# Low target blocks of a graph network's last five layers: sums by gathered rows beside the dense products

## The reference

```python
# second layer (l1 in the kernel): both directions of each edge, unit weights
src2, dst2 = concat([src, dst, loop]), concat([dst, src, loop])
agg = segment_sum(x[src2] * dis[src2] * dis[dst2], dst2);  x = layernorm(x + relu(agg @ W.T + bias))
# third (l2): one direction, unit weights
out = segment_sum((x @ W)[row] * dinv[row] * dinv[col], col) + b;  x = layernorm(x + prelu(out))
# fourth to sixth (l3a, l3b, l3c): one direction, edge weights; 128 -> 256 -> 256 -> 128 features
h = relu(conv(x, W1));  h = relu(conv(h, W2));  x = layernorm(x + conv(h, W3))
```

## Time and profile before

| what | value |
|---|---|
| median of 3 runs | 5592.74 us (5584.71 to 5594.79) |
| time of the profiled execution | 5637.0 us |
| its span from first to last instruction | 5635.2 us |
| TensorE (PE) busy | 4813.6 us, 85% |
| VectorE (DVE) busy | 2493.0 us, 44% |
| GpSimd (POOL) busy | 1199.1 us, 21%, all but 5 us in the first layer |
| moved to and from HBM | 1178.49 MB, 209 GB/s |
| granted clock of TensorE over the span | 0.910 of full speed |

### The profile page before, as it was taken

One profiled execution on the slowest core, in us unless ns is written; L12 is line 12 of the kernel. 1 busy time (PEld: TensorE's weight loads), 2 busy tenths in 40 slices (PEclk: granted clock), 3 DMA queues, 4 the chain that ended last, 5 costly groups with the idle time before them and its releaser, 6 DMA issues. The chain is left out here.

```text
span 5635.2 us, 75975 instructions
## 1 busy us (share of the span) xinstructions
PE 4813.6 (85%) x30664; PEld 3047.7 (54%) x30664; DVE 2493.0 (44%) x4225; ACT 1157.3 (21%) x2219; POOL 1199.1 (21%) x845
## 2 busy tenths in 40 slices
PE   3788888888888863388879989999999999999999
PEld 2777777777777753233334444444444444454444
DVE  5877888888788767755542220111000000001111
ACT  0555555555555541100000000000000000000000
POOL 2655656566666610000000000000000000000000
PEclk6888988889898876689989999999999999999999
DMA  4665666666666651288876658887444444338887
GB/s 139 204 199 188 218 198 202 205 202 216 199 213 213 201 179 55 94 299 294 298 225 206 212 187 305 305 306 263 150 155 144 147 149 155 140 132 289 310 306 261
DMA packets 689173, 1178.49 MB, mean 209 GB/s; under 512 B 77284, under 2 KB 450384, under 8 KB 688440
## 3 DMA queue, kind: packets, MB, share of 16 engines
q1 hardware_dynamic: 617004, 1079.58, 55.6%
q0 software_dynamic: 26864, 55.10, 3.9%
q10 hardware_dynamic: 44956, 38.94, 2.2%
HBM read 823.64 MB, written 349.75 MB: 208 GB/s over the span
## 5 line engine op out<-in xcount | busy, mean ns | idle before, releaser
L756 POOL DMA_INDIRECT x<-p_table,src_i x832 | 1191.9, 1433 | 801.6 <-DVE x L553 516.3
L1197 PE MATMUL po_l3b<-mat_l3b,rows_b 128*128 128x512 f32 (+1 forms) x2548 | 1042.5, 569 | 12.2 <-DMA mat_l3b<-weights_fwd 12.2
L740 ACT CAST st_cnt<-ps_mat 128x512 bf16<-128x512 f32 x1225 | 661.2, 585 | 749.4 <-PE ps_deg L665 373.4
L1197 PEld LDWEIGHTS po_l3b<-mat_l3b,rows_b 128*128 128x128 f32 x2548 | 467.6, 191 | 555.7 <-issue 542.4
L675 PE MATMUL ps_mat<-rows_a,hot_s 128*128 128x128 bf16 x7203 | 593.0, 240 | 100.1 <-issue 45.9
L660 PE MATMUL ps_mat<-rows_a,hot_s 128*128 128x128 bf16 x2401 | 396.5, 231 | 230.1 <-issue 81.4
L675 PEld LDWEIGHTS ps_mat<-rows_a,hot_s 128*128 128x128 bf16 x7203 | 482.5, 109 | 162.9 <-ACT st_wt L744 83.2
L1197 PE MATMUL po_l<-mat_l,rows_a 128*128 128x512 bf16 (+1 forms) x1911 | 429.6, 387 | 152.2 <-DVE mat_l L1365 152.2
L541 DVE TENSOR_TENSOR rows_a<-rows_a,slots 128x1536 bf16<-128x1536 bf16 (+1 forms) x294 | 543.5, 1885 | 2.4 <-issue 0.2
L1197 PE MATMUL po_l3a<-mat_l3a,rows_a 128*128 128x512 f32 (+1 forms) x1274 | 523.5, 570 | 16.2 <-DMA mat_l3a<-weights_fwd 16.2
L1197 PE MATMUL po_l3c<-mat_l3c,rows_a 128*128 128x512 f32 (+1 forms) x1274 | 522.1, 569 | 11.8 <-DMA mat_l3c<-weights_fwd 11.7
(11 more groups left out here) (334 smaller groups left out, 4777.3 us busy)
## 6 DMA issues: line engine op xcount, KB each, us to landing
weights_fwd<-st_wt SPq DMA_DIRECT2D x588, 256.0 KB
mat_l<-counts_fwd SPq DMA_DIRECT2D x168, 896.0 KB, 5.4
mat_l3a<-weights_fwd SPq DMA_DIRECT2D x84, 1792.0 KB, 7.1
mat_l3b<-weights_fwd SPq DMA_DIRECT2D x84, 1792.0 KB, 7.1
mat_l3c<-weights_fwd SPq DMA_DIRECT2D x84, 1792.0 KB, 7.1
counts_fwd<-st_cnt SPq DMA_DIRECT2D x588, 128.0 KB
counts_rev<-st_cnt SPq DMA_DIRECT2D x588, 128.0 KB
rev_l<-counts_rev SPq DMA_DIRECT2D x84, 896.0 KB, 7.9
```

What stands on the lines that cost most here:

```text
L740: nc.scalar.copy(st_cnt[:, q, :, j * 2 * P:j * 2 * P + n_col], ps_mat[:, f % 3, :].rearrange("p (d c) -> p d c", d=2)[:, :, 0:n_col]).then ...
L756: pool.indirect_dma_start(ring[:, j % RING, t * FD:(t + 1) * FD], None, p_table, bass.IndirectOffsetOnAxis(src_i[:, j * TH + t:j * TH + t ...
L1197: mm = nc.tensor.matmul(po[:, g % 2, k, 0:nb * P].rearrange("p (d c) -> p d c", c=P), rows[:, s, k * P:(k + 1) * P], mat[:, n % slots, 0:n ...
```

## The change

In each of the five layers the first 12 target blocks (20 in l3b), which are 3 (5) of the 13 groups, are no longer summed by the forward matrices. Their edges are summed in half-steps, as in the first layer: 52 half-steps (86 in l3b), each of 4 gathers of 128 rows, one-hot matrices on VectorE (with edge weights in l3a to l3c), 4 float32 products (8 in l3b) and an addition into `acc`. The half-steps are spread over the chunks of the other groups, at most one to a chunk (two in l3b). `products` is the order of the dense groups: the one-block group first, then the groups behind the low ones. In l1 the low groups still have products with the reverse matrices, at the end and without `add_rev`, since the forward part comes from the half-steps. In the other layers the low groups' `take`, `conv` and `finish` run beside the last products ("along"). `EARLY` is 2 in place of 3. `rec` has 8 fields in place of 6, and separate ones for the edges that the half-steps cover. `finish` comes behind chunk 3 as before (chunk 2 in l3b, with `finish_wide` behind chunk 3), `turn` in l3b behind chunk 2 and `widths` behind chunk 3.

```diff
+LOWS = (12, 20)
+PER_GROUP = 17
+EARLY_BY, LATE_BY = 1, 18
...
+            low_n, low_js, low_loc, low_at = LOWS[lows], low_steps[lows], low_local[lows], low_first[lows]
+            low_groups = list(range(low_n // GB))
+            products = [GROUPS - 1] + list(range(low_n // GB, GROUPS - 1))
+            if both:
+                products += low_groups
+            dense = len(products) - (len(low_groups) if both else 0)
+            along = {}
+            if not both:
+                for q in low_groups:
+                    along[dense - len(low_groups) + q] = q
...
+            FIRST, SECOND = 1, 4
+            weights = [min(GB, NB - g * GB) if p else 0 for p, g in enumerate(products[:dense]) for _ in range(CHKS)]
+            usable = sum(weights) - (0 if both else (CHKS - SECOND + 1) * weights[-1])
+            beside = [[] for _ in range(dense * CHKS)]
+            so_far = 0
+            for n, w in enumerate(weights):
+                so_far += w
+                done = sum(len(js) for js in beside)
+                beside[n] = [j for j in range(done, min(low_js, so_far * low_js // usable))]
...
+            RL = 3 if two else 4
+            HL = 2 if two else 4
+            pas = 1 if kind in ("hidden", "hidden2") else 2
...
+                        for j in range(low_js):
+                            if j >= RL:
+                                wait_apart(pool, step_sum, j - RL + 1, passed)
+                            for t in range(TH):
+                                pool.indirect_dma_start(
+                                    ring[:, j % RL, t, :], None, table,
+                                    bass.IndirectOffsetOnAxis(low_src[:, j * TH + t:j * TH + t + 1].bitcast(U32), 0)
+                                ).then_inc(gathered[j % RL], 16)
...
+                        def half_step(j):
+                            pe.wait_ge(hot_ready, j + 1)
+                            pe.wait_ge(gathered[j % RL], 16 * TH * (j // RL + 1))
+                            if j >= pas:
+                                pe.wait_ge(added, j - pas + 1)
+                            for k in range(K):
+                                for t in range(TH):
+                                    mm = nc.tensor.matmul(pa[:, j % pas, k * W:(k + 1) * W],
+                                                          ring[:, j % RL, t, k * P:(k + 1) * P], hot[:, j % HL, t, :],
+                                                          start=(t == 0), stop=(t == TH - 1))
+                            mm.then_inc(step_sum, 1)
...
+                        for p in range(len(products) + 1):
                             for ch in range(CHKS):
+                                if p < len(products):
+                                    chunk(p, ch)
+                                if p == 0 and ch == EARLY - 1:
                                     rest()
+                                if p < dense:
+                                    for j in beside[p * CHKS + ch]:
+                                        half_step(j)
+                                for f, piece in at_task(p, ch):
+                                    if piece == 0:
+                                        conv(f)
+                                    if two and piece == 1:
+                                        turn(f)
+                                    if two and piece == 2:
+                                        widths(f)
...
+                        def add_sums(j):
+                            at = dve.value_load(low_at[0:1, j:j + 1], min_val=0, max_val=low_n * P)
+                            if j:
+                                dve.wait_ge(added, j)
+                            dve.wait_ge(step_sum, j + 1)
+                            to = acc[:, :, bass.ds(at, W)]
+                            V.tensor_tensor(to, to, pa[:, j % pas, 0:K * W].rearrange("p (k c) -> p k c", c=W),
+                                            ALU.add).then_inc(added, 1)
...
+                        for p in range(len(products) + 1):
+                            if p < len(products):
+                                own_rows(with_products[p + 1][0] if p == 0 or len(with_products[p]) < 2 else with_products[p][1])
                             for ch in range(CHKS):
+                                if p < dense and both:
+                                    add_rev(p, ch)
+                                if p == 0 and ch == EARLY - 1:
                                     rest()
+                                if p < dense:
+                                    for j in beside[p * CHKS + ch]:
+                                        if j + HL // 2 < low_js:
+                                            low_hots(j + HL // 2)
+                                        add_sums(j)
+                                for f, piece in at_task(p, ch):
+                                    if piece == 0:
+                                        take(f, (p - 1) % 2)
+                                    if piece == (1 if two else 2):
+                                        finish(f)
+                                    if two and piece == 2:
+                                        finish_wide(f)
```

More of the change, by code:

```diff
@@ L1211, in own_part, with conv @@
                             mm.then_inc(summed, 1)
-                        def conv(g):
-                            pe.wait_ge(taken, g + 1)
-                            if g >= pcs:
-                                pe.wait_ge(conv_read, g - pcs + 1)
-                            for d in range(blocks_in(g)):
-                                o = pc[:, g % pcs, d * Fo:(d + 1) * Fo]
+                        def conv(f):
+                            pe.wait_ge(taken, f + 1)
+                            if f >= pcs:
+                                pe.wait_ge(conv_read, f - pcs + 1)
+                            if two and f:
+                                pe.wait_ge(turned_read, f)
+                            for d in range(blocks_in(tasks[f])):
+                                o = pc[:, f % pcs, d * Fo:(d + 1) * Fo]
@@ new lines, in take @@
+                            dve.wait_ge(left_in[f % 2], 16 * (f // 2 + 1))
+                            s = sums[:, f % 2, :, 0:nb * P]
+                            mark = V.tensor_tensor(s, po[:, b, :, 0:nb * P], left[:, f % lefts, :, 0:nb * P], ALU.add)
+                            if is_low(g):
+                                chain.step(mark)
+                                dve.wait_ge(added, low_js if both else min(low_js, PER_GROUP * g + LATE_BY))
+                                mark = V.tensor_tensor(s, s, acc[:, :, g * GB * P:(g * GB + nb) * P], ALU.add)
@@ L1433, in _ @@
+                        chain.step(V.memset(acc[:], 0.0))
+                        for j in range(HL // 2):
+                            low_hots(j)
+                        for p in range(len(products) + 1):
+                            if p < len(products):
+                                own_rows(with_products[p + 1][0] if p == 0 or len(with_products[p]) < 2 else with_products[p][1])
                             for ch in range(CHKS):
-                                if both and g < GROUPS:
-                                    add_rev(g, ch)
@@ new lines, in _ @@
+                                for f, piece in at_task(p, ch):
[5 more added lines that the diff above has]
+                                        finish_wide(f)
+                                if p and p < len(products) and len(with_products[p]) > 1 and ch == SECOND:
+                                    own_rows(with_products[p + 1][0])
```

388 lines of the change are left out of this document (236 added, 152 removed).

## The result

The changed kernel took 5673.3 us in the median of 4 runs (5660.9 to 5684.0), the kernel before 5593.8 us on the same chip (5584.7 to 5605.1): ratio 1.014, 95% interval 1.0113 to 1.0168. It is 80 us slower, where 31 us less was predicted. The time lies inside the range, on the other side of no change.

What follows compares the result with a forecast made beforehand. It took l2 to l3c as bound by TensorE's products, l1 by waits for VectorE's additions and their loads. +41 + 220 - 23 - 56 - 157 - 56 = -31 us gave 5562 us, range 5490 to 5710.

Steps and rivals of the forecast that it cites:

- Records, +41: Behind the first layer, some 37 chained operations and a longer store of the records add 41 us.
- l1, +220: In l1 VectorE's additions wait for TensorE's half-steps, ending the overlap: 804 us against 584, so +220.
- That term, 72 us: In l1 the clock falls after stalls: 1.1 us for 46 of them, 2.4 for the 9 behind `finish`.
- B: Rival: the short stalls of l1 leave the clock alone, 50 us less: -81, 5512 us; chance 0.15.
- C: Rival: every stall of l1 halves the clock for the next chunk, in all +29, 5622 us; chance 0.13.
- l2, -23: In l2: products gone -97, half-steps +47, waits +12, starts and ends +10, clock +5, together -23 us.
- l3a and l3c, -56 each: Each: products gone -128, half-steps +47, waits +12, starts and ends +10, 3 given back for loads: -56 us.
- l3b, -157: In l3b: products gone -425, half-steps +154, waits +84, starts and ends +10, clock +20, together -157 us.
- Clock: I add 5, 0, 20 and 0 us: Clock loss for stalls over 2 us in l2, l3a, l3b and l3c, in that order.
- -31: Sum of the forecast's terms for the whole kernel: 31 us faster, 5562 us.
- D: Rival: the gathers don't keep up in l2, l3a and l3c, +151, 5744 us; chance 0.22.
- E: Rival: l1 doesn't couple, VectorE stays ahead and l1 gets 40 us faster: -291, 5302 us; chance 0.05.

Runs made afterwards that it cites:

- e7: Changed kernel with no low blocks in any layer (all products dense), records kept, one-block group last again: 5424.0 us against 5386.4, ratio 1.0064.
- e8_all: Changed kernel with `add_rev` of the next chunk (l1), `take` and `finish` (every layer) ahead of the half-steps' sums: 5055.3 us against 5386.4, ratio 0.9407.
- e2: Changed kernel, but in l1 VectorE adds the next chunk's reverse matrices ahead of the half-step's sums: 5491.4 us, ratio 0.9799 to the kernel before.
- e12: Changed kernel, unaltered, run again on the chip of the last set: 5424.0 us against 5388.7 for the kernel before, ratio 1.008.
- e3: Changed kernel, but `take` and `finish` stand ahead of the half-steps' sums in l2, l3a, l3b and l3c: 5510.2 us, ratio 0.9817 to the kernel before.
- e10_best_wide: Changed kernel with l1 dense, `take` and `finish` ahead of the sums elsewhere, 128-column half-step products in l3b: 5034.0 us against 5388.7, ratio 0.935.
- e5: Changed kernel, but l3b's half-step products have 128 columns, the second result not used: 5655.4 us, ratio 1.0108 to the kernel before.
- e11: Changed kernel with l1 dense and its one-block group last again, `take` and `finish` ahead of the sums elsewhere: 5050.5 us against 5388.7, ratio 0.939.
- e1: Changed kernel, but l1 has no low blocks and keeps all its dense products: 5456.7 us against 5610.2 for the kernel before, ratio 0.9723.
- e6: Changed kernel with no low blocks in any layer, records kept, one-block group still first: 5465.4 us against 5386.4 for the kernel before, ratio 1.0154.

## Why the prediction was wrong, point by point

- **Records, +41:** right (+40 in the trace, +38 us in e7).
- **l1, +220:** right, in size and in mechanism (+215). The stall of 2.5 us is 2.42 in the cycle shown. The cycle of 8.1 us is at full clock; the one shown took 9.7 us, for the clock. That term, 72 us, measures about 64: TensorE's busy time for the same products is 550.4 us here and 486.5 in e8_all, which itself stands at the lower level for 103 us of l1. It is near the forecast's value between rivals B (the short stalls cost nothing) and C (each costs 2.4 us): of the 37 stalls of 2.4 to 2.8 us, 26 are followed by the lower level within a chunk and 11 are not. The Trainium skill, "TensorE: Matmul & The Clock Gate", section "HAM oscillation", tells of waits of about 3 to 5 us before each tile. These stalls are shorter, so the section does not speak for C. The trace shows what it does not say: waits of 2.4 us bring the clock down too, but not each time. e2's order saves nine tenths of l1's loss.
- **l2, -23, measured +6: wrong.** Three terms were too small. Waits for VectorE at `conv` were put at 12 us and measure 21 (20.6 and 2.3 of "issue", less the 2.2 that were there). The clock was put at 5 us; busy time is 382.3 against 366.8 us in e8_all, 15. And 12 us of "issue" gaps at the one-block group in front were not foreseen; in e12, without them, l2 takes 414.2 us, 17 us less than the dense layer of e7. Waits and gaps share the clock's part: l2 stands at the lower level for 62 us with both, for 42 in e3 (gaps alone), 35 in e12 (waits alone) and 20 in e8_all (neither), the last two on other chips.
- **l3a and l3c, -56 each:** right within 1 and 8 us.
- **l3b, -157, measured -86: this is the step that failed.** The products that went (-425) and the waits (84 predicted, 94 by the trace: 96 less the 2 of before) were right. What failed is "Clock: I add 5, 0, 20 and 0 us ... for the stalls over 2 us". With the clock whole, in e10_best_wide, the same instructions keep TensorE busy for 880 us, 5 of them for the wider passes; in the changed kernel 945. So the clock costs 70 us, not 20. Two things were missing. A pair of half-steps with 0.64 us between was priced by its passes alone, as work at full clock that leaves the clock as it is; the row used for it, has the duration of narrow products but not what follows them. And stalls of 2 to 4 us just behind such a pair lower the clock for the next chunk as well: e3, which removes the stalls alone, wins 49 us of busy time, and e5, which widens the products alone, 33 (what each wins contains what the two cost only together). These 50 us, 10 for the waits and 8 for the first loads (20.5 us in place of 12.2) are 68 of the 71 us that l3b lacks.
- **The sum.** 71 us of l3b, 29 of l2 and 8 of l3c, less 6 elsewhere, turn -31 into +71. The other 9 of the measured 80 us lie ahead of that stretch or in the spread between executions. In e12 the same kernel is only 35 us slower, with layers 45 us shorter. The time lies inside the range by its width and not by its reasons: D's full price is 5744 us by the forecast's own sum, which the upper end of 5710 leaves out.
- **The rivals.** D (gathers don't keep up) did not happen: they took 1122 ns in the mean over l1 and l2 together (1258 and 986), 1011 and 978 in l3a and l3c and 977 in l3b, 208 and 344 a layer, and none of the half-steps' products (L1327) waited for one:

```profile
L1291 POOL DMA_INDIRECT rows_b<-x_table,low_src x416 | 466.8, 1122 | 533.5 <-PE pa_l L1327 387.3
...
L1291 POOL DMA_INDIRECT rows_a<-h_table,low_src x344 | 336.0, 977 | 607.9 <-PE pl_l3b L1327 514.3
```

  GpSimd was idle for longer than it worked, waiting for TensorE to free the ring. D's argument against itself, that the slow gathers belong to VectorE's bfloat16 work, fits l1, the one layer that has this work: the 70 of its gathers that overlap an addition of reverse matrices take 1.86 us in the mean and the other 138 take 0.95. One of either kind, and the addition:

```profile
2603.70 2.02 DVE L1551 TENSOR_TENSOR mat_l<-mat_l,rev_l 128x3584 bf16<-128x3584 bf16 x1
2604.14 2.40 POOL L1291 DMA_INDIRECT rows_b<-x_table,low_src  x1 [1.81 <-PE pa_l L1327]
2606.84 0.94 POOL L1291 DMA_INDIRECT rows_b<-x_table,low_src  x1 [0.30 <-issue]
```

  E (no coupling) did not happen; in e2, where most of the coupling is gone, l1 takes 605.5 us and not 40 us less than before. Of B and C neither: the clock of l1 went as forecast. The largest cause behind the turned sign, some 60 us of clock in l2 and l3b beyond the forecast, stood there as terms of 5 and 20 us and in no rival.
- **Not seen:** that one cause stood behind most of the listed costs. The text priced the waits of `add_rev`, `take` and `finish` one by one. All three come from an operation that waits for TensorE's current chunk (`add_sums`) placed ahead of work that TensorE's next chunk needs, and without it the same gathers make the kernel 331 us faster than before.

**What stays open.** Why the short products come with gaps in some runs and not in others was not settled. In the five traces of the first two chips, every l1 and l2 with half-steps has 11 to 18 us of "issue" waits at the dense products; in those of the other two chips none has them. Whether the pause of 0.64 us in each pair (26 us in all) can go was not tried, so whether 64 columns lower the clock without any pause is not shown.

## What to carry to other kernels

When work is added beside a product stream, the place of its receiving operation in the other engine's program matters more than its cost: put everything that the next chunk needs ahead of the operation that waits for the current chunk (here moving `add_rev`, `take` and `finish` turned a loss of 35 to 80 us into a gain of 331). Price added products not only by their duration but by what they do to the granted clock for the work behind them. And skip layers whose bound is not what the change removes: l1 lost 215 us and had nothing to win.

## What the runs showed of the hardware that was not expected

- Products of 64 columns (16 in 1.97 us, their weight loads 1.86 us of it) let the clock fall though TensorE was busy for 3.66 of 4.3 us, at 9 to 14 of the 41 pairs in the runs without the longer stalls: the next 28 products took 13.93 us instead of 12.18. With 128 columns, a second half thrown away, 16 passes took 2.02 us with the same pause between, and the clock stayed at all 41 pairs. The extra columns cost next to nothing and bring 17 us (e11 to e10) to 34 us (changed kernel to e5) in l3b.
- Chips differ. The kernel before took 5594 us beside the result and 5610, 5386 and 5389 us beside the three sets. Nearly all of it is the first layer: the last product into `ps_deg` starts at 2040.5 us in the result's run, at 2061.7 in e1 and at 1820.5 in e6. The same change measures 1.014 on one chip and 1.008 on another.
- In some runs a dense stretch of short products comes one to five at a time with gaps of mostly 1 us that no wait explains (12 us in l2 and as much in l1).
- An indirect gather that GpSimd issued during VectorE's bfloat16 addition of 2.02 us took 2.40 us, the next one 0.94.
